# Folding a cross-attention's projections: m kept in SBUF for all batches, key and query parts unstacked, u in packed jobs of 128 rows

## What is computed

```python
# x: (4, 2048, 512)   context: (4, 77, 512)   16 heads of 64
xn = layernorm(layernorm(x)) * ln_gamma + ln_beta
q = xn @ w_q                                 # (512, 1024)
k, v = split(context @ w_kv)                 # (512, 2048)
attn = softmax(q_h . k_h / 8)                # per head, over 77 keys
x = x + tanh(g_xattn) * tanh(gate) * (concat_h(attn_h v_h) @ w_out + b_out)
y = layernorm(x)
# top 2 of 10 gates (8 experts, 2 null), weights renormalized over the true ones
x = x + tanh(g_ffn) * sum_e combine[t, e] * (y @ expert_w[e] + expert_b[e])
```

## Time and profile before

| | us |
|---|---|
| median of 3 runs | 1451.48 |
| lowest and highest run | 1450.27, 2309.28 |
| span of the profiled execution | 1433.4 |
| median less span | 18.1 |
| PE, DVE, ACT, POOL busy in the span | 1308.8, 1142.2, 792.0, 711.0 |

### The profile page before, as it was taken

The page is one execution under the profiler, slowest core; times in us unless marked ns, Lnnn a source line. Parts: engine busy times, 40 slices in busy tenths (PEclk is TensorE's granted clock), DMA queues, the critical chain, the costliest instruction groups (busy, mean ns, idle before and its releaser), DMA issues. The chain is left out here.

```text
span 1433.4 us, 30500 instructions
## 1 busy us (share of the span) xinstructions
PE 1308.8 (91%) x7199; PEld 674.3 (47%) x7200; DVE 1142.2 (80%) x2911; ACT 792.0 (55%) x2839; POOL 711.0 (50%) x648
## 2 busy tenths in 40 slices
PE   5576799999999999999999999995789987999997
PEld 3432355555555555555555555552344543444553
DVE  5876788899999999999999999987466665666665
ACT  5775666666666666666666666662443332434442
POOL 0270123244554554554455455446666665666764
PEclk9797999999999999999999999998799999999999
DMA  5895678899997798987798977785355545677773
GB/s 196 199 265 169 191 159 198 196 210 232 222 221 185 183 228 211 240 204 185 186 234 204 256 186 189 181 175 165 83 140 150 149 130 178 217 225 229 246 243 98
DMA packets 434765, 278.03 MB, mean 194 GB/s; under 512 B 340477, under 2 KB 368189, under 8 KB 434542
## 3 DMA queue, kind: packets, MB, share of 16 engines
q1 hardware_dynamic: 406830, 202.76, 58.7%
q0 software_dynamic: 27840, 74.18, 16.5%
HBM read 121.27 MB, written 82.58 MB: 142 GB/s over the span
## 5 line engine op out<-in xcount | busy, mean ns | idle before, releaser
L866 PE MATMUL scores<-m_sb,zT 128*128 (+2 forms) x2304 | 414.4, 338 | 6.1 <-PEq L158 6.1
L981 ACT ACTIVATE expd<-scores,less 128x77 f32<-128x77 f32 x1024 | 317.4, 328 | 181.8 <-DVE less L1085 180.7
L881 PE MATMUL mix<-u_sb,pT 128*128 128x512 f16 x1728 | 383.5, 379 | 1.1 <-issue 0.6
L1839 PE MATMUL out_bank<-w_parts,m_sb 128*128 x1440 | 333.5, 382 | 3.7 <-DVE token_out L1945 2.4
L866 PEld LDWEIGHTS scores<-m_sb,zT 128*128 128x128 f16 x2304 | 220.5, 98 | 172.7 <-issue 8.2
L881 PEld LDWEIGHTS mix<-u_sb,pT 128*128 128x128 f16 x1728 | 169.0, 98 | 198.2 <-issue 0.7
L981 ACT ACTIVATION_READ_ACCUMULATOR expd<-scores,less 128x1 f32 x1024 | 213.4, 208 | 0.0
L1839 PEld LDWEIGHTS out_bank<-w_parts,m_sb 128*128 128x128 f16 x1440 | 141.8, 98 | 150.6 <-issue 9.7
L1555 POOL DMA_INDIRECT table<-payload,row_i x128 | 160.2, 1251 | 60.5 <-issue 37.9
L1864 ACT CAST m_sb<-yT_bank 128x512 f16<-128x512 f32 x120 | 70.2, 585 | 207.9 <-PE yT_bank L1826 100.7
L1452 POOL TENSOR_TENSOR z_parts<-z,z_parts 128x512 f16<-128x512 f32 x62 | 71.7, 1156 | 192.2 <-ACT z_parts L972 192.2
(11 more groups left out here) (181 smaller groups left out, 1758.1 us busy)
## 6 DMA issues: line engine op xcount, KB each, us to landing
comb<-x_out SPq DMA_DIRECT2D x64, 512.0 KB, 3.2
x_ln<-in_x_dram SPq DMA_DIRECT2D x64, 256.0 KB
x_res<-in_x_dram SPq DMA_DIRECT2D x64, 256.0 KB
w_raw<-in_L_ffn_expert_w_dram SPq DMA_DIRECT2D x64, 128.0 KB, 2.3
m_dram<-m_stage SPq DMA_DIRECT2D x32, 231.0 KB, 4.5
u_dram<-m_sb SPq DMA_DIRECT2D x48, 154.0 KB
m_sb<-m_dram SPq DMA_DIRECT2D x12, 616.0 KB
u_sb<-u_dram SPq DMA_DIRECT2D x6, 1024.0 KB, 7.7
```

The lines of the kernel that those rows point to most:

```text
L866: last = pe.matmul(scores[s][k][:, 0:n], zT[:, s, zp, t, :], m, start=(t == 0 and (zp, mp) == PRODUCTS[0]), stop=(t == DT - 1 and (zp, mp) ...
L881: last = pe.matmul(mix[:], pT[:, s, pp, k, :], u_sb[:, k, up, :], start=(k == 0 and (pp, up) == PRODUCTS[0]), stop=False)
L981: last = act.activation(expd[:, s, h * KEYS:(h + 1) * KEYS], scores[s][k][:, at:at + KEYS], ACT.Exp, bias=less[:, s, h:h + 1], scale=1.0 / ...
L1839: last = pe.matmul(c.out_bank[s][:], yT[:, s, yp, t, :], w_parts[:, bass.ds(e, 1), t, wp, :].rearrange("p a n -> p (a n)"), start=(t == 0 ...
```

## The change

m of all four batches stays in SBUF: one tensor `arena` of five regions, each as large as one batch's m. `m_all`, regions 1 to 4, is written by the m jobs directly. `w_parts` takes regions 0 to 3: the expert weights that are split during batch b go into region b, which held m of the batch before. `m_dram`, `m_stage`, `load_m` and their semaphores and waits are gone. During the fold, the arena's later-written parts hold the raw chunks and their parts, so that all w_kv and w_q chunks have a place of their own; w_out is loaded as two chunks of four pairs into u_sb's room.

`k_parts` and `wq_parts` hold a pair of heads in 128 partitions, high and low apart, one copy per engine and job. An m job is three matmuls over the 64 partitions of its head; the two heads of a pair are issued alternately into two banks.

v is written as a block diagonal, `v_block`: head 2m+a of a pair in the half a of the partitions and in its own 77 columns, zeros elsewhere (a memset on POOL). A job of u is then 128 consecutive rows of the 1232 (the last one 80): 10 jobs per batch, 40 in all, each with three matmuls for every pair of heads that its rows touch, the later pair first. Jobs of batch 0 write into `u_sb` itself, but for the last; the other 31 go through `u_stage`. In attention SP waits for u's stores between steps 0 and 1.

```diff
-    MEASURED, NORMALIZED, SPLIT, TURNED, THIRD = 8, 16, 32, 44, 48
+    MEASURED, NORMALIZED, SPLIT, TURNED, THIRD = 4, 10, 18, 26, 30
-    NU = BATCH * HEADS
+    NU = BATCH * KT
...
             if n < V0:
-                return twice(k_twice, n - K0, bank[:, 0:CK], K_SCALE / (C_SCALE * W16))
+                m = n - K0
+                return [(k_parts[:, 0, m], k_parts[:, 1, m], k_parts[:, 0, m], bank[:, 0:CK], K_SCALE / (C_SCALE * W16))]
             if n < WQ0:
-                return stacked(v_stack, n - V0, bank[:, 0:CK], K_SCALE / (C_SCALE * W16))
+                m = n - V0
+                return [(by_head(v_block, 0, m, a), by_head(v_block, 1, m, a), by_head(v_block, 0, m, a),
+                         bank[HALVES[a], 0:CK].rearrange("p (b j) -> p b j", b=BATCH), K_SCALE / (C_SCALE * W16))
+                        for a in range(2)]
             if n < M0:
-                return stacked(wq_stack, n - WQ0, bank[:], W16)
+                m = n - WQ0
+                return [(wq_parts[:, 0, m], wq_parts[:, 1, m], wq_parts[:, 0, m], bank[:], W16)]
...
+            _, k, rows = u_job(n - U0)
+            q = staged(n - U0)
+            to = u_sb[:, k] if q is None else u_stage[0:rows, q % US]
+            return [(to[:, 0], to[:, 1], to[:, 0], bank[0:rows, :], u_gain[0:rows, :])]
...
-            for c in range(RAW):
-                load_chunk(c)
-
-            for c in range(WQ_CHUNK, WQ_CHUNK + 4):
-                sp.wait_ge(chunk_lo_ready, c - RAW + 1)
-                load_chunk(c)
+            for c in range(KV_CHUNKS):
+                load_columns(raw_kv[c], wkv, c, kv_in[c])
+            for c in range(WQ_CHUNKS):
+                load_columns(raw_wq[c], wq, c, wq_in[c])
+            sp.wait_ge(product_ready, K0)
+            for c in range(WOUT_CHUNKS):
+                sp.dma_start(raw_wout[:, c * PER_CHUNK:(c + 1) * PER_CHUNK],
+                             wout[c * PER_CHUNK * P:(c + 1) * PER_CHUNK * P, :].rearrange("(m p) n -> p m n", p=P)).then_inc(
+                                 wout_in[c], 16)
...
-            for g in range(NM // 4):
-                dt, quad = divmod(g, 4)
-                sp.wait_ge(hi_ready, M0 + 4 * g + 4)
-                sp.wait_ge(lo_ready, M0 + 4 * g + 4)
-                cols = slice(quad * 4 * KEYS, (quad + 1) * 4 * KEYS)
-                sp.dma_start(m_sb[:, 0, dt, :, cols], m_stage[:, g % MS, 0]).then_inc(m_stored[g % MS], 16)
-                for part in range(2):
-                    sp.dma_start(m_dram[1:, :, dt, part, cols].rearrange("b p c -> p b c"),
-                                 m_stage[:, g % MS, 1:, part]).then_inc(m_stored[g % MS], 16)
...
+            for n in range(0, NM, 2):
+                t, h = divmod(n, HEADS)
+                m = h // 2
+                if t == 0:
+                    pe.wait_ge(hi_ready, WQ0 + m + 1)
+                    pe.wait_ge(lo_ready, WQ0 + m + 1)
+                outs = [bank(M0 + n), bank(M0 + n + 1)]
+                for wp, kp in PRODUCTS:
+                    for a, half in enumerate(HALVES):
+                        last = pe.matmul(outs[a][:, 0:CK], wq_parts[half, wp, m, t * P:(t + 1) * P], k_parts[half, kp, m, :],
+                                         start=((wp, kp) == PRODUCTS[0]), stop=((wp, kp) == PRODUCTS[-1]))
+                        if (wp, kp) == PRODUCTS[-1]:
+                            last.then_inc(product_ready, 1)
...
+                for m in range((k * P + rows - 1) // PAIR_KEYS, k * P // PAIR_KEYS - 1, -1):
+                    mine = min(rows, (m + 1) * PAIR_KEYS - k * P)
+                    for vp, wp in PRODUCTS:
+                        last = pe.matmul(out[0:mine, :], v_block[:, vp, b, k * P:k * P + mine], wout_parts[:, m, wp, :],
+                                         start=((vp, wp) == PRODUCTS[0]), stop=((vp, wp) == PRODUCTS[-1]))
+                        if k == 0 and (vp, wp) == PRODUCTS[0]:
+                            for part in range(2):
+                                pe.matmul(out[0:KEYS, :], ones_row[:], bias_parts[:, part], start=False, stop=False)
...
+        ORDER = ( ... jobs(K0 + 4, K0 + 8) + [("chunk", 3)] + jobs(K0 + 8, M0 + 8) + [("chunk", 4)]
+                 + jobs(M0 + 8, M0 + 20) + [("chunk", 5)] + jobs(M0 + 20, U0 + NU))
...
+            pool.memset(v_block[:].rearrange("p l b c -> p (l b c)").bitcast(F32), 0.0).then_inc(v_clear, 1)
...
                 step(i0, 0)
+                if first:
+                    for u_stored, stores in zip(ln.u_stored, ln.u_stores):
+                        sp.wait_ge(u_stored, stores)
+                        sp.nop(nofuse=True)
                 step(i0 + 1, 1)
...
-                if not last and not first:
-                    sp.wait_ge(scores_ready, 3 * i0)
-                    sp.nop(nofuse=True)
                 for k in range(4):
-                    if not last:
-                        load_m(sp, m_sb[:, bass.ds((b + 1) % 2, 1)], m_dram, b + 1, k).then_inc(m_in, 16)
                     step(i0 + TPB - 4 + k, k % 2)
...
-                            m = m_sb[:, bass.ds(i // TPB % 2, 1), t, mp, c0:c0 + n].rearrange("p a c -> p (a c)")
+                            m = m_all[:, bass.ds(i // TPB, 1), t, mp, c0:c0 + n].rearrange("p a c -> p (a c)")
...
-        y = rows_of(0, TURNS)
-        biased = rows_of(TURNS, TURNS)
-        result = rows_of(2 * TURNS, R)
+        y = sb("expert_y", [P, TURNS, D], F32)
+        biased = sb("biased", [P, TURNS, D], F32)
+        result = sb("result", [P, R, D], F32)
+        yT = sb("expert_yT", [P, TURNS, 2, DT, P], F16)
```

More of the change, by code:

```diff
@@ new lines, in u_pieces, with u_stores @@
+            return [(stage[0:LAST, 0:1].broadcast_to([LAST, 2, D]), u_sb[0:LAST, k]),
+                    (stage[0:ROOM, 1], u_sb[LAST:P, k, 0]),
+                    (stage[ROOM:LAST, 1], u_sb[LAST:LAST_LO, k, 1])]
+        def u_stores(slot, last):
+            return 16 * sum(len(u_pieces(n)) for n in range(NU) if staged(n) in range(slot, last + 1, US))
+        def stage_free(engine, n):
+            q = staged(n - U0) if n >= U0 else None
+            if q is not None and q >= US:
+                engine.wait_ge(u_stored[q % US], u_stores(q % US, q - US))
```

242 lines of the change are left out of this document (95 added, 147 removed).

## The result

| | before | after | ratio, 95% interval |
|---|---|---|---|
| first pair, median us | 1451.43 | 1409.51 | 0.972, 0.968 to 0.976 |
| lowest and highest run | 1450.27, 2309.28 | 1404.69, 1415.04 | |
| profiled execution, span us | 1433.4 | 1413.3 | |

The changed kernel is faster by 2.8%, 41.9 us between the medians; 1415.5 us had been forecast, with a range of 1405 to 1430. The ratio leaves out the run of before at 2309.28 us, a slow one. The profiled execution of after is the 1415.04 us run, the slowest of its four. Its span is 1413.3 us, so only 1.7 us lie around it; the other three runs show 1.7 to 1.8 us too. A ratio from the two profiled spans, 1413.3/1433.4 = 0.986, would have been half of the effect.

The account below looks back on a forecast made before the run. TensorE fills attention, so time can move in the fold, where it waits on ACT/DVE copies and DMA stores. Terms -7.4 - 6.9 - 9.4 - 12.3 = -36.0 us take the 1451.5 us median to 1415.5; range 1405 to 1430.

Parts of the forecast that it names:

- Keys, values and wq: First fold stretches: fewer, full-height bank copies; -7.4 us for keys and values, a further -6.9 us for wq.
- m: Fold's m stretch: store waits go, DVE's 64 copies bind, ending at 82.4 us instead of 106.09; -9.4 us.
- u: Fold's u stretch: 40 copies, 212 products, PE becomes the bound; end 130.1 us instead of 166.06; -12.3 us.
- 2.3 us for a cold start and changes of shape: Added in u for a start at less than full clock and for changes of shape between products; 2.3 us.
- The slots and stores: In u, 33 stores and the reuse of slots were taken to cost 0, with 3 us as upper bound.
- the 18.1 us "around the span": Whole run: difference between before's profiled span, 1433.4, and its median, 1451.5; left unchanged in the forecast.
- span 1397.4: Profiled execution of the changed kernel: span forecast to go from 1433.4 to 1397.4 us.
- A: Rival in u: PE does not get its full clock (0.84); +9 us, 1424.5 us; chance 0.17.
- B: Rival in m: 64-row products expose their weight loads; +18.4 us, 1434 us; chance 0.10.
- C: Rival in u: half clock throughout; the prediction's text gives no description or size; chance 0.04.
- D: Rival in attention: the 36 us come back as waits, through the new wait on u_stored; 1451 us; chance 0.03.
- The cost per change of shape: In u: some 48 changes at 0.08 us each cost 3.8 us instead of 2.3; 1417 us for the whole.

Follow-up runs that it names:

- ring5: Before with a fifth group in the m_stage ring instead of four; 1408.47 us in one run, before 1412.37 on that chip.
- copies: After with before's copies put back: keys copied out four times and wq transposes twice, in halves; 1389.25 us in one run.
- heads_apart: After with each head's three m products issued together instead of alternating between the two heads of a pair; 1411.27 us over 2 runs.
- wide: After with no product group of u under 65 output rows, some u values wrong, product count unchanged; 1408.94 us over 2 runs.
- before_again: Before, unedited, run and profiled a second time; 1451.6 us over 10 runs, ratio to before 0.9994.
- stores: After with m also stored to DRAM, three stores per group, nobody waiting for them before the fold's end; 1373.02 us on the second chip.

## Why the prediction was right, and where it wasn't

Stage by stage, in us from the start of the profiled execution:

| the step | forecast | measured |
|---|---|---|
| last key or value product | 46.9 | 47.1 |
| last wq copy of DVE | 54.5 | 53.9 |
| last m copy of DVE | 82.4 | 80.3 |
| PE starts on u | 79.6 | 77.8 |
| last u copy of DVE | 130.1 | 130.5 |
| attention starts | 131.7 | 131.5 |
| attention takes | as before | 819.3 to 821.0, before and ring5 820.7 to 821.9 |

The 807 us that the prediction names as attention's length is the window of the earlier trace rows, which was cut at 975 us; the stage takes 820.7 us in before. The forecast doesn't hang on it.

**Keys, values and wq** were right in mechanism and size, and copies shows it. That the last product came within 0.2 us is partly luck: the forecast took over the 14.98 us of before's first 96 products, 18 of them 0.256 us apart, and other executions of after end this stretch 1.3 and 1.4 us earlier. The copies of 128x512 on DVE came 0.61 us apart, not the 0.708 of the 64x512 ones; that is the 0.6 us.

**m** came 2.1 us early: 0.6 by inheritance, 1.0 as DVE's 64 copies took 24.9 us instead of 25.9, and 0.5 as the chunk splits cost DVE 1.5 us and not 2. PE's 192 products weren't the bound, since the halves run side by side (heads_apart); at full clock a pair starts 0.77 us after the one before it, for it waits on DVE's two copies of 0.389. At the lower clock PE had nothing to spare.

**u** has the one mis-sized term of the fold. PE took 51.1 us from its first product to the end of its last (77.81 to 128.93), not 49.2. The forecast had 2.3 us for a cold start and changes of shape. The clock was 1.00 throughout and the first products of u stand at their usual distance, so nothing went to the start, and the changes cost 48 x 0.10 = 4.8 us (wide), while a product took 0.216 instead of 0.221: 212 x 0.216 + 4.8 = 50.6. This error of +1.9 and the -1.8 of the earlier start cancelled. The slots and stores cost nothing, as assumed.

**What failed is the last term, the 18.1 us "around the span".** They aren't around it. 1.7 to 1.8 us are, in every run whose span is known, of before too; so the profiled execution of before must have been shorter than its timed runs, by some 16 us. Its experts' stage was: 445.1 us there and 460.5 when before was profiled again. The sum span + rest came out near the median all the same, since the forecast left those 18.1 us alone, and that is the right thing to do with a difference that the change doesn't touch, whatever its name. But the prediction gave it a place where it isn't, and its own check "span 1397.4" missed by 15.9 us (1413.3): a reader who compares spans would have called the change half as good as it is.

**The 6 us between forecast and median.** 1415.5 - 1409.5. The gain was 36.0 by forecast and 41.9 by the first medians, 41.3 and 39.5 us when measured again (1451.6 to 1410.33, 1448.87 to 1409.34). In the trace of before_again the fold is 2.4 us longer than in that of before, with ACT waiting 10.8 us for m_dram and not 9.1:

```profile
L460 ACT ACTIVATE m_stage<-fold 128x308 f16<-128x308 f32 x64 | 22.7, 450 | 12.3 <-DMA m_dram<-m_stage 10.8 <-PE fold L408 0.9
```

so the fold's gain is 36.2 to 39.5 us, depending on which execution of before one takes; attention gave 1.4 us in the first pair and 0.1 in the second. 4.3 us of the medians' difference are left in the first pair and 1.7 in the second; they are within the scatter of the stages and aren't attributed.

**The rivals.** A (part clock in u): false, 1.00 in every stretch of u; the 0.84 of before was that of a PE busy for 39 of 60 us. B (64-row products expose their weight loads): false, a pair's six products take 0.57 us from first start to last end and run side by side. C (half clock through u): false with A. D (the gain comes back in attention): false, attention took 819.3 to 821.9 us in every kernel, with the new wait ahead of step 1 or without it. The cost per change of shape that the prediction had tried at 0.08 us was there and was 0.10; the whole came out below the 1417 it had named nonetheless, by the other terms.

## What to carry to other kernels

Price a change stage by stage from the rows, at the last engine of each stretch, and look for one thing beside it: whether the profiled execution is a typical one. When span and median differ by more than the few us that lie around a span, some stage of that execution was shorter or longer than usual, and spans of two kernels must not be compared before it is found. A ring that waits for its stores costs the wait and not the traffic: one more group bought 2.5 us of the stretch here, keeping the data 11. And full-height jobs pay for copies saved even where TensorE gets more products, but each change between narrow and full-width output has its price and belongs in the sum.

## What the hardware showed that I had not expected

- Two 64-row products on different halves of the array's rows run side by side even when the queue has three of one half ahead: their starts are 13 to 24 ns apart in heads_apart.
- A change between groups with up to 54 and with 65 or more output rows costs TensorE 0.10 us, either way; 78, 80 and 104 against 128 cost nothing. Where between 54 and 65 the line is was not measured.
- Copies of a full bank out of PSUM are priced by columns: on DVE one of 64x512 lasts 688 ns by its record (copies) and one of 128x512 683 ns (after), or 748 ns where it takes u's gain as an operand as well. In a row the halves stand 0.709 us apart and the full ones 0.61. Nor do the 77 rows of before's u copies (738 ns) save anything against 128.
- Traffic at a DMA share of 1.07 beside DVE and ACT copies left their durations as they were (stores).
- The experts' stage, the same work in both kernels, takes 418 to 421 us on one chip and 445 to 463 in the other executions, so that it can hide or add to the gain of this change in a comparison of single spans.
- The first 10 to 23 products of the key stretch run at half pace, 0.256 us apart and not 0.131, while the profile's granted clock reads 1.00. How many there are differs between executions of one kernel (23, 12 and 11 in after) and moves the end of that stretch by up to 1.4 us.
